# A four-engine order of steps for the middle tiles of a two-layer network, written in another way

## The reference

```python
x = x + _L0_attn_ref(_layernorm(x), ...)   # linear attention, 16 heads, phi(x) = silu(x) + 1, no softmax
x = x + _L0_ffn_ref(_layernorm(x), ...)    # 256 -> 1024: silu(w1 x) * (w2 x); gelu(h1 .); gelu(h2 .); w3: 1024 -> 256
x = x + _L1_attn_ref(_layernorm(x), ...)   # softmax attention, one head of 256, 512 x 512 scores
x = x + _L1_ffn_ref(_layernorm(x), ...)    # three 256 x 256 products in a row, then tanh(. + bias)
```

## Time and profile before

| | us |
|---|---|
| median of 3 runs | 2042.87 |
| lowest and highest | 2038.68, 2043.28 |
| profiled execution, its own time | 2039.22 |
| span of its instructions | 2037.5 |

### The profile page before, as it was taken

The page is one execution under the profiler, slowest core; times in us unless marked ns, Lnnn a source line. Parts: engine busy times, 40 slices in busy tenths (PEclk is TensorE's granted clock), DMA queues, the critical chain, the costliest instruction groups (busy, mean ns, idle before and its releaser), DMA issues.

```text
span 2037.5 us, 37348 instructions
## 1 busy us (share of the span) xinstructions
PE 1988.6 (98%) x15484; PEld 1918.9 (94%) x15484; DVE 1237.9 (61%) x2881; ACT 792.3 (39%) x1502; POOL 379.5 (19%) x347
## 2 busy tenths in 40 slices
PE   5999999999999999999999999999999999999996
PEld 4999999999999999999999999999999999999985
DVE  5645666566575656666466675656666566664465
ACT  2334335253443434435253343434335353342332
POOL 2011211122121121210222121121210212111111
PEclk8999999999999999999999999999999999999999
DMA  9600000000000000000000000000000000000000
GB/s 348 219 4 1 22 1 1 22 1 22 1 22 1 1 22 1 22 1 1 22 1 22 1 15 7 1 22 1 22 1 1 22 2 11 1 8 5 1 1 21
DMA packets 24453, 46.01 MB, mean 23 GB/s; under 512 B 1184, under 2 KB 21408, under 8 KB 24096
## 3 DMA queue, kind: packets, MB, share of 16 engines
q1 hardware_dynamic: 24272, 43.41, 6.1%
HBM read 35.02 MB, written 19.92 MB: 27 GB/s over the span
## 4 chain that ended last, share of the span: by engine, by line
PE 91%; DVE 5%; issue 2%; POOL 1%; ACT 0%; DMA 0%; POOLq 0%; DVEq 0%; ACTq 0%
PE ffn_fill L981 47%; PE att_fill L931 26%; PE ffn_fill L931 9%; PE ffn_fill L1039 6%; PE att_fill L999 1%; PE att_fill L1116 1%; DVE st L630 1%; DVE xn L643 1%; POOL rstd_C L599 1%; PE ffn_fill L1007 1%; DVE whole L697 1%; DVE x L715 0%; DVE xn_b L712 0%; DVE mv_C L634 0%; DVE late_xn L643 0%
## 5 line engine op out<-in xcount | busy, mean ns | idle before, releaser
L981 PE MATMUL ffn_fill<-act_hi,h 128*128 128x256 f32 x4096 | 986.4, 283 | 0.2
L981 PE MATMUL ffn_fill<-act_lo,h 128*128 128x256 f32 x4096 | 979.4, 281 | 0.0
L981 PEld LDWEIGHTS ffn_fill<-act_lo,h 128*128 128x128 f32 x4096 | 772.2, 189 | 4.8
L981 PEld LDWEIGHTS ffn_fill<-act_hi,h 128*128 128x128 f32 x4096 | 771.4, 188 | 5.4 <-POOL act_lo L613 0.8
L869 ACT ACTIVATE whole<-ffn_fill,scales 128x256 f32<-128x256 f32 x512 | 213.0, 472 | 429.1 <-PE ffn_fill L981 428.1
L706 DVE CAST act_hi<-whole 128x512 fp32r<-128x512 f32 x256 | 108.4, 424 | 270.8 <-ACT whole L869 269.2
L931 PE MATMUL ffn_fill<-half_hi,w 128*128 128x256 f32 x1024 | 254.0, 288 | 9.1 <-DVE whole L697 4.5
L931 PE MATMUL ffn_fill<-half_lo,w 128*128 128x256 f32 x1024 | 249.6, 283 | 0.0
L613 POOL TENSOR_TENSOR act_lo<-whole,act_hi 128x512 fp32r<-128x512 f32 x128 | 169.9, 1332 | 295.6 <-DVE act_hi L702 295.1
L931 PEld LDWEIGHTS ffn_fill<-half_hi,w 128*128 128x128 f32 x1024 | 195.5, 191 | 13.2 <-DVE whole L697 7.6
L931 PEld LDWEIGHTS ffn_fill<-half_lo,w 128*128 128x128 f32 x1024 | 196.2, 192 | 0.6
(11 more groups left out here) (218 smaller groups left out, 3270.4 us busy)
## 6 DMA issues: line engine op xcount, KB each, us to landing
x<-in_L_attn_x SPq DMA_DIRECT2D x16, 512.0 KB, 3.6
out<-x SPq DMA_DIRECT2D x16, 512.0 KB, 3.0
h<-scratch_h1T SPq DMA_DIRECT2D x2, 2048.0 KB, 10.5
h<-scratch_h2T SPq DMA_DIRECT2D x2, 2048.0 KB, 11.4
w<-scratch_w1T SPq DMA_DIRECT2D x1, 1024.0 KB, 9.5
w<-scratch_w2T SPq DMA_DIRECT2D x1, 1024.0 KB, 10.5
w<-scratch_w3T SPq DMA_DIRECT2D x1, 1024.0 KB, 26.2
rows<-in_rows SPq DMA_DIRECT2D x1, 640.0 KB, 5.9
```

Of the source, the lines that this page charges most:

```text
L981: last = pe.matmul(two(bank)[:, o, :], view(w), view(moving[:, k, :]), start=k == 0 and o == 0 and half == 0, stop=k == KH - 1 and half == ...
```

## The change

In BODY all four engines get another order of the same steps. No step is added or taken away, and no instruction of a step differs. PLAN stays, and so do the banks and the semaphore values. FIRST and END stay.

```diff
@@ PE_ORDERS
     "BODY": order_from("""
-    U0 U1 U2 U3a c:T U3b G0a c:CV c:CZ G0b G1a c:CS0 G1b G2 c:CP0 c:CS1 G3a c:CS2 G3b c:CO0 c:CP1 H0a c:CS3
-    H0b c:CO1 c:CP2 H1a c:CO2 c:CP3 H1b H2 c:CO3 H3 BT1 W0 U0a c:T U0b U1 c:CF a:T U2 U3a a:AKV0 a:AKV1
-    a:AKV2 a:AKV3 U3b G0a a:AS a:AQa G0b a:AQb G1 G2 a:AM G3 a:AOa H0 a:AOb H1 H2 H3 n:BT0 W1"""),
+    U0 U1 U2 U3 G0 G1a c:T G1b G2a c:CV c:CZ G2b c:CS0 G3 c:CP0 c:CS1 c:CS2 c:CO0 H0a c:CP1 c:CS3 H0b c:CO1
+    c:CP2 H1a c:CO2 H1b c:CP3 H2 c:CO3 H3 BT1 W0 U0a c:T U0b U1 c:CF U2a a:T U2b U3 G0a a:AKV0 a:AKV1 a:AKV2
+    a:AKV3 G0b G1 G2 a:AS a:AQ a:AM G3 a:AO H0 H1 H2 H3 n:BT0 W1"""),
@@ DVE_ORDERS
     "BODY": order_from("""
-    c:CST U0 c:CNO U1 c:T U2 U3 c:CQ c:CV c:CZ c:CS0 G0 c:CP0 c:CS1 c:CS2 G1 G2 c:CO0 G3 c:CP1 c:CS3 c:CO1
-    c:CP2 c:CO2 BST1 H0 c:CP3 H1 BNO1 a:AST c:CO3 H2 c:DST H3 BT1 c:DNO W0 c:T a:ANO c:CF U0 a:T U1 a:AKV0
-    a:AKV1 a:AKV2 a:AKV3 U2 U3 a:AS G0 a:AQ a:AM G1 G2 G3 a:AO n:BST0 n:BNO0 H0 H1 H2 H3 n:BT0 W1"""),
+    U0 U1 U2 U3 c:CST c:CNO c:T G0 c:CQ c:CV c:CZ G1 c:CS0 c:CP0 c:CS1 G2 c:CS2 G3 c:CO0 c:CP1 c:CS3 c:CO1
+    c:CP2 H0 c:CO2 BST1 c:CP3 H1 BNO1 a:AST c:CO3 c:DST H2 H3 BT1 c:DNO W0 c:T U0 a:ANO c:CF U1 a:T U2 U3
+    a:AKV0 G0 a:AKV1 a:AKV2 a:AKV3 a:AS G1 G2 a:AQ a:AM a:AO G3 n:BST0 n:BNO0 H0 H1 H2 H3 n:BT0 W1"""),
@@ ACT_ORDERS
     "BODY": order_from("""
-    U0 U1 U2 c:T U3 c:CV c:CZ G0 c:CS0 G1 G2 c:CP0 c:CS1 c:CS2 G3 c:CP1 c:CS3 c:CP2 H0 c:CP3 H1 H2 H3 BT1
-    c:T U0 U1 c:CF a:T U2 a:AKV0 U3 a:AKV1 a:AKV2 a:AKV3 a:AQ G0 a:AM G1 G2 G3 H0 H1 H2 H3 n:BT0"""),
+    U0 U1 U2 U3 G0 c:T c:CV c:CZ G1 G2 c:CS0 c:CP0 G3 c:CS1 c:CS2 c:CP1 c:CS3 c:CP2 H0 c:CP3 H1 H2 H3 BT1 U0
+    c:T U1 c:CF a:T U2 U3 a:AKV0 a:AKV1 a:AKV2 G0 a:AKV3 G1 G2 a:AQ a:AM G3 H0 H1 H2 H3 n:BT0"""),
@@ POOL_ORDERS
     "BODY": order_from("""
-    c:CST U0 U1 c:CB U2 U3 BST1 a:AST c:DST U0 c:CF U1 a:AB U2 U3 n:BST0"""),
+    U0 U1 U2 U3 c:CST c:CB BST1 a:AST c:DST U0 c:CF U1 U2 a:AB U3 n:BST0"""),
```

## The result

| | before | after |
|---|---|---|
| median of 14 runs, us | 2041.04 | 2033.15 |
| lowest and highest, us | 2037.11, 2043.45 | 2030.12, 2035.78 |
| span of the profiled execution, us | 2037.5 | 2030.0 |
| a middle round (mean of 13), us | 122.87 | 122.33 |

The ratio after to before is 0.9963, with a 95% interval of 0.9955 to 0.9972: 7.6 us faster. A round is measured from one W step to the W step 13 rounds later in the chain of work: before 277.60 to 1874.95, after 275.71 to 1866.04.

What follows compares the result with a forecast made beforehand. PE, busy 98% of the span, was taken as the bound, with its waits. The terms -11.7 + 3.9 + 2.4 gave -5.4 us, so a median of 2036.0 us, within a range of 2029 to 2048.

Steps and rivals of the forecast that it cites:

- the rival in which all edges hold: Only the 0.28 us in G0 is paid each round: -7.8 us, 2035.1 against the median; chance 0.20.
- the likeliest case: The forecast itself, for the whole kernel: faster by 1 to 7 us; chance 0.50.
- The wait at c:T: First half, around c:T and U3: PE's wait for DVE's U1 multiplication (L697) goes, 0.90 us in 13 rounds, 11.7 us.
- The new wait in G0: G0's last quarter waits for U3's low part from POOL: 0.28 us in each of 14 rounds, 3.9 us.
- xn ready for c:T: At c:T's new place in G1, xn's fourth block is ready by 0.5 us; costed at nothing.
- c:CS0, 0.05 us taken: Softmax start behind half of G2: a wait for c:CZ's low part, between nothing and 0.3 us; 0.05 taken.
- c:CP0, 0.02 taken: Behind G3: a wait for the exponential, between nothing and 0.3 us; 0.02 taken.
- a:T and G0's second quarter in the second half: Waits for c:CF's second bank (up to 0.3 us, 0.07 taken) and POOL's U1 (up to 0.5, 0.03 taken).
- the rival of the shared port: Second half: DVE and POOL stop each other, new waits of 0.88 us a round, +0.6 us in all; chance 0.14.
- The rival of the longer softmax chain: First half, c:CP0: the chain outlasts G3, PE loses 1.2 us a round, +9 us, 2048; chance 0.09.
- The rival in which c:T waits again: xn comes 0.8 us late at c:T, 0.4 to 0.9 us return each round, 2039 to 2046; chance 0.07.
- The level of the time: Whole kernel: three earlier runs seemed to fall at two levels, so the median was set between 2033.8 and 2037.5 us.

Runs made afterwards that it cites:

- The first half alone: The kernel before with the new orders up to W0 and the old ones behind; 0.9964 of the kernel before, a round of 122.31 us.
- The version without any wait: The changed kernel with U3's low part on DVE, c:CZ ahead of c:CV, three statistics behind U0, U1, U2; 0.9947 of the kernel before, median 2028.82 us.
- the second half alone: The kernel before with the old orders up to W0 and the new ones behind; 1.0004 of the kernel before, a round of 122.90 us.

## Why the prediction was right

It said 2036.0 us and a gain of 5.4; measured are 2033.15 and 7.6. In a round it said -0.45 and the trace has -0.54. The two large terms, 0.90 and 0.28, were right and read from rows. The small ones were guesses between nothing and some tenths, and together too large: of 0.17 us a round 0.05 was paid for sure. So the gain came out next to the rival in which all edges hold (7.8 us, a chance of 0.20) and a little beyond the likeliest case (1 to 7 us, 0.50); 5.4 lies outside the interval of 5.7 to 9.2. By its steps:

- The wait at c:T, 0.90 us a round. Right in place and size. The first half alone brings all of it, and the swap of U1 and xn shows that the place of xn on DVE made it. The version without any wait has a round of 122.01 us, 0.86 less than before.
- The new wait in G0, 0.28 us. Right: 0.29 in the trace. It was read from the end of the kernel, where the order stood already, and it took 3.9 of the 11.7 us.
- xn ready for c:T with 0.5 us to spare. Right, and shown from the other side: with 0.69 us more on DVE and 0.29 less on PE, thus 0.98 less cover, c:T lost 0.55, of which 0.11 is the restart. That leaves 0.54 us of cover.
- c:CS0, 0.05 us taken. Right, the trace has 0.05; putting c:CV between took it away.
- c:CP0, 0.02 taken. None in the trace: the chain behind c:CS0 ends 3.49 us after PE's end there (918.06 to 921.55), as it was before with 3.48, and 0.40 us more in it made PE wait.
- a:T and G0's second quarter in the second half, 0.07 and 0.03 taken. No wait in the trace. The second half costs 0.03 us a round at most, and the runs don't say where. This is where the sum was too careful. POOL did come between the blocks of xn there, which is what the rival of the shared port held. The rows, DVE first, then POOL:

```profile
956.62 0.87 DVE L697 SCALAR_TENSOR_TENSOR whole<-ffn_fill,scales,gated 128x256 f32<-128x256 f32 x2
957.86 2.36 DVE L643 TENSOR_SCALAR xn<-x,mv_A,rstd_A 128x256 f32<-128x256 f32 x4
960.14 1.41 DVE L793 TENSOR_TENSOR kv_b<-att_fill,rows 128x256 f32<-128x256 f32 x4
...
958.03 1.40 POOL L613 TENSOR_TENSOR act_lo<-whole,act_hi 128x512 fp32r<-128x512 f32 x1 [9.07 <-DVE act_hi L702]
964.06 1.30 POOL L613 TENSOR_TENSOR act_lo<-whole,act_hi 128x512 fp32r<-128x512 f32 x1
```

The blocks took 2.36 us, and yet a:T at 961.36 was not late. The four additions of c:CF took 1.41 us together, not 4 × 0.42, since they overlap by 0.09 each, and each step before them began a little ahead of the last one's end. So the second bank was free some 0.4 us ahead of PE. POOL's U1 ended at 965.36, and G0's second quarter begins at 965.06 + 0.95 = 966.01. The mechanism of that rival was there, its price was not.

- The rival of the longer softmax chain (slower) needed one more table load in the chain or a late DVE. Neither is there: the trace has one load between the bias and the exponential, and DVE's maximum starts 0.20 us after PE's end (918.26), as it did before. Nor is there a drain behind the load: it runs from 919.47 to 920.75, and the exponential starts at 920.77.
- The rival in which c:T waits again had a slip in its sum. The 0.8 us already had the 0.5 of cover taken off, and its lower bound took it off once more. No run turns on it, since POOL was free in time.
- The level of the time was read from three runs that seemed to lie at two levels. In 14 runs there are no two levels: they lie between 2037.1 and 2043.5 us without a gap of over 1.4, with the median at 2041.04. So the 2042.87 of the prediction was high by 1.8.

The sum by rounds: 13 × 0.54 = 7.0 us, less 0.34 for the first round, which had no wait before and has the two new ones: 6.7 us. That is inside the interval of the ratio, 5.7 to 9.2 us.

## What to carry to other kernels

When one engine is the bound and a wait is moved away from it, look for the next hand-over that has lost its cover. If the same order already stands somewhere in the kernel, read its price there: it came out within 0.01 us here. Work out each hand-over from PE's end to the weights of the step that asks, with every bank and every part that the step needs, since the one forgotten bank cost 0.49 us a round. And don't pack DVE's steps so close that each cast falls under a subtraction of POOL, which made it 0.84 us here instead of 0.43. Into the gap of 0.55 us went one statistics instruction of 0.42 at a time, not the whole block.

## What the runs showed that I had not expected

The clock of PE at the start of the middle. The same window of before and then of after (length, busy us and instructions of PE, its weight loads, DVE, ACT and POOL, granted clock, DMA share, GB/s):

```profile
157.00:162.00 5.00, 4.41 (x24) 4.45 (x25) 2.54 (x11) 0.84 (x2) 1.01 (x1) 0.66 0.01 3
```

```profile
157.00:162.00 5.00, 5.00 (x43) 5.00 (x44) 2.27 (x6) 1.73 (x5) 1.30 (x1) 1.00 0.01 3
```

In both, PE stops for 2.3 to 2.4 us ahead of it. In the trace of before the granted clock is then 0.66 as a mean, with some 15 matmuls 0.21 us apart instead of 0.12, the lower of its two levels; in that of after it stays full. This doesn't go with the change: most other versions with the new orders show 0.66 to 0.68, and the one with the second half alone, whose U steps are those of before, shows 1.00. Without the stop ahead of it, the first round took 123.76 us before and 122.56 after. The clock is more than all of that 1.2 us, since 15 matmuls that each take 0.09 us longer are 1.4, and the first round after has the two new waits. The end of the kernel went the other way: from its first U step to the end of the span it is 158.8 us before and 160.2 after, and the same 38 us of its work had a mean clock of 0.89 before (1998.9 to 2036.9) and 0.76 after (1990 to 2028). A comparison of two spans has such pieces in it, and that of the rounds hasn't. Whether they are all of the 2037 to 2043 us over which the runs of one kernel spread is left open.
